# A post-norm decoder layer on one core: row norms moved to ScalarE, recurrence scans joined in pairs, and attention scores of the first rows in two matmuls in place of three

## Time and profile before

| | before |
|---|---|
| median of 3 runs | 1664.29 us (1663.91 to 1665.35) |
| profiled execution, its own time | 1663.39 us |
| its span | 1661.6 us |
| busy PE / PEld | 1571.6 us (95%) / 1424.5 us (86%) |
| busy VectorE | 1389.3 us (84%) |
| busy ScalarE / GpSimd | 1064.8 us (64%) / 995.3 us (60%) |
| granted PE clock, mean | 0.991 |

### The profile page before, as it was taken

How to read it: one execution, slowest core, us unless ns; L and a number is a source line. 1 busy time by engine, 2 the same in 40 slices (tenths; PEclk the granted TensorE clock), 3 DMA queues, 4 the chain that set the end, 5 groups by cost and what they waited for, 6 DMA issues and landing times.

```text
span 1661.6 us, 32864 instructions
## 1 busy us (share of the span) xinstructions
PE 1571.6 (95%) x10720; PEld 1424.5 (86%) x10720; DVE 1389.3 (84%) x3314; ACT 1064.8 (64%) x2883; POOL 995.3 (60%) x856
## 2 busy tenths in 40 slices
PE   5899999999999999999999999999999977989897
PEld 4899989898999999899989998989898966778785
DVE  4555699899989998989899989898989896977874
ACT  4777676767676767676767676767676754233322
POOL 3555566666666666666666666666656652645652
PEclk9999999999999999999999999999999999999999
DMA  7766344424442444244424451445134522112121
GB/s 237 265 197 210 108 134 147 134 58 146 147 134 59 146 146 134 58 140 134 153 56 127 133 169 44 127 139 173 43 121 147 176 57 83 51 66 82 69 77 51
DMA packets 83144, 202.62 MB, mean 122 GB/s; under 512 B 11808, under 2 KB 12832, under 8 KB 82976
## 3 DMA queue, kind: packets, MB, share of 16 engines
q1 hardware_dynamic: 82976, 200.53, 38.6%
HBM read 120.80 MB, written 37.75 MB: 95 GB/s over the span
## 4 chain that ended last, share of the span: by engine, by line
PE 69%; DVE 17%; issue 7%; ACT 3%; POOL 2%; DVEq 1%; SPq 1%; DMA 0%; ACTq 0%; POOLq 0%
PE bank L490 21%; PE bank L492 20%; PE bank L491 20%; PE bank L604 4%; DVE QS L1204 2%; DVE A L1220 2%; DVE PS L1211 1%; DVE S L1069 1%; DVE PTl L1058 1%; DVE RC L1085 1%; PE bank L595 1%; PE bank L587 1%; DVEq L1293 1%; DVE RO L1137 1%; DVE E L1192 1%
## 5 line engine op out<-in xcount | busy, mean ns | idle before, releaser
L490 PE MATMUL bank<-Xh,W 128*128 128x256 f32 x1280 | 362.6, 283 | 36.1 <-DVE RC L1085 26.3
L492 PE MATMUL bank<-Xh,W 128*128 128x256 f32 x1280 | 358.5, 280 | 0.0
L491 PE MATMUL bank<-Xl,W 128*128 128x256 f32 x1280 | 357.7, 279 | 0.0
L946 POOL TENSOR_TENSOR Ql<-RC,Qh 128x512 fp32r<-128x512 f32 x128 | 167.6, 1309 | 266.0 <-ACT Qh L692 265.8
L490 PEld LDWEIGHTS bank<-Xh,W 128*128 128x128 f32 x1280 | 242.1, 189 | 42.9 <-DVE RC L1085 24.2
L692 ACT ACTIVATE PTh<-bank 128x384 fp32r<-128x384 f32 x256 | 125.2, 489 | 211.1 <-PE bank L604 210.7
L692 ACT ACTIVATE S<-S,RL 128x128 f32<-128x128 f32 (+1 forms) x512 | 204.3, 448 | 82.9 <-DVE RL L1077 82.2
L707 ACT ACTIVATE S<-S,NM 128x128 f32<-128x128 f32 (+1 forms) x512 | 227.8, 446 | 40.4 <-DVE NM L1069 39.7
L492 PEld LDWEIGHTS bank<-Xh,W 128*128 128x128 f32 x1280 | 243.0, 190 | 0.0
L491 PEld LDWEIGHTS bank<-Xl,W 128*128 128x128 f32 x1280 | 242.2, 189 | 0.0
L936 POOL TENSOR_TENSOR SW<-SW,tables 128x512 f32<-128x512 f32 x128 | 168.2, 1314 | 116.7 <-DMA SW<-QB 116.2
(11 more groups left out here) (144 smaller groups left out, 4344.2 us busy)
## 6 DMA issues: line engine op xcount, KB each, us to landing
W<-kept SPq DMA_DIRECT2D x140, 512.0 KB, 4.5
SW<-QB SPq DMA_DIRECT2D x256, 128.0 KB, 2.3
kept<-W SPq DMA_DIRECT2D x40, 512.0 KB, 4.5
XR<-in_xt SPq DMA_DIRECT2D x16, 512.0 KB, 4.0
XR<-XR SPq DMA_DIRECT2D x64, 128.0 KB, 2.4
RO<-in_xn SPq DMA_DIRECT2D x16, 512.0 KB, 3.9
KVT<-in_ctxt SPq DMA_DIRECT2D x16, 512.0 KB, 4.3
mixed<-RO SPq DMA_DIRECT2D x16, 512.0 KB, 3.7
```

The lines of the kernel that those rows point to most:

```text
L490: nc.tensor.matmul(dst, lhs[0], rhs[0], start=first, stop=False)
L491: nc.tensor.matmul(dst, lhs[0], rhs[1], start=False, stop=False)
L492: return nc.tensor.matmul(dst, lhs[1], rhs[0], start=False, stop=last)
L946: gp.tensor_tensor(Q[1][:, :, :], RC[:, i % 2, :, :], Q[0][:, :, :], ALU.subtract).then_inc(q_lo, 1)
```

## The change

**Scores.** K's high and low part stand side by side in one tile `KHL`. For rows 0 to 127 one matmul with Q's high part as weights and 2 x 128 columns (128 of K high, 128 of K low) writes columns 0 to 255 of the bank; one with Q's low part adds K high x Q low into columns 0 to 127. The part high x low stays apart in columns 128 to 255. `three` for rows 128 to 255 writes columns 256 to 511. VectorE gets a new instruction per head: the columns 128 to 255 plus mask into S (`masked`); the reduction of the first tile then adds columns 0 to 127 to that, and comes last, after the second tile's.

**Norms.** `norm_apply` goes. VectorE makes -mean*rstd for both row tiles in one 128x2 instruction (`norm_shift`), and ScalarE applies scale and shift in two activations per norm, at the end of the slots with lag 1 and lag 19.

**Scans.** A2, E2, PS and QS have rows of 257 columns with a zero in front, and one scan runs over two channel tiles (514 columns): the zero factor at the border restarts it. Two QS and two PS scans per tail in place of four and four. The memset of PS goes.

**Order.** In odd slots `maxima` stands after the accumulator read; GpSimd's bias adds (line 960) are spread over slots 7, 9 and 11, 13 in place of 9, 11 and 11, 11.

```diff
+QS_AT, PS_AT, ED_AT = [(8, 0), (10, 0)], [(10, 1), (12, 0)], [(6, 0), (9, 0)]
...
-        K = [sb(f"K{i}", [P, 2, JL, T], fr) for i in "hl"]
+        KHL = sb("KHL", [P, 2, JL, 2, T], fr)
+        K = [KHL[:, :, :, i, :] for i in range(2)]
...
+        A2Z = sb("A2Z", [P, KC, T + 1])
+        E2Z = sb("E2Z", [P, KC, T + 1])
+        A2, E2 = A2Z[:, :, 1:T + 1], E2Z[:, :, 1:T + 1]
...
+        in_row = lambda a, h: two(a, h).rearrange("p k t -> p (k t)")
...
-                    for t, c0, keys in ((0, 0, P), (1, P, T)):
-                        last = three(s_ps[:, c0:c0 + keys], [a[:, q, t * P:(t + 1) * P] for a in Q],
-                                     [a[:, par, j, 0:keys] for a in K])
-                    last.then_inc(scored, 1)
+                    nc.tensor.matmul(s_ps[:, 0:2 * P].rearrange("p (i k) -> p i k", i=2), Q[0][:, q, 0:P], KHL[:, par, j, :, 0:P], start=True, stop=False)
+                    nc.tensor.matmul(s_ps[:, 0:P], Q[1][:, q, 0:P], K[0][:, par, j, 0:P], start=False, stop=True)
+                    three(s_ps[:, T:2 * T], [a[:, q, P:T] for a in Q], [a[:, par, j, :] for a in K]).then_inc(scored, 1)
...
+                def norm(kind, tau, rs, nm, done):
+                    act.wait_ge(shifted, SHIFTS.index((kind, tau)) + 1)
+                    rows = RO[:, ro_buf(TAIL_BATCH[tau]), :, :]
+                    for t in range(TT):
+                        last = nc.scalar.activation(rows[:, t, :], rows[:, t, :], ACT.Identity,
+                                                    bias=nm[:, tau % 2, t:t + 1], scale=rs[:, tau % 2, t:t + 1])
+                    last.then_inc(done, 1)
...
-                    b = rows_of(n, 9 + 2 * t, 11)
+                    b = rows_of(n, 7 + 2 * t, 11 + 2 * t)
...
-                    for t, c in ((0, slice(0, P)), (1, slice(P, P + T))):
-                        last = v.tensor_tensor_reduce(out=S[:, i, c], in0=s_ps[:, c], in1=Mask[:, c], scale=-SCALE,
-                                                      scalar=3e38, op0=ALU.add, op1=ALU.min, accum_out=NM[:, i, t:t + 1])
-                    last.then_inc(maxed, 1)
+                    v.tensor_tensor(S[:, i, 0:P], s_ps[:, P:T], Mask[:, 0:P], ALU.add).then_inc(masked, 1)
+                    v.tensor_tensor_reduce(out=S[:, i, P:P + T], in0=s_ps[:, T:2 * T], in1=Mask[:, P:P + T], scale=-SCALE,
+                                           scalar=3e38, op0=ALU.add, op1=ALU.min, accum_out=NM[:, i, 1:2])
+                    dve.wait_ge(masked, g + 1)
+                    v.tensor_tensor_reduce(out=S[:, i, 0:P], in0=s_ps[:, 0:P], in1=S[:, i, 0:P], scale=-SCALE,
+                                           scalar=3e38, op0=ALU.add, op1=ALU.min, accum_out=NM[:, i, 0:1]).then_inc(maxed, 1)
...
-                    last = v.tensor_scalar(tiles[:, t, :], tiles[:, t, :], mv[:, par, t, 0:1], rs[:, par, t:t + 1],
-                                           ALU.subtract, ALU.mult)
+            def norm_shift(par, mv, rs, nm):
+                v.scalar_tensor_tensor(out=nm[:, par, :], in0=mv[:, par, :, 0], scalar=-1.0, in1=rs[:, par, :],
+                                       op0=ALU.mult, op1=ALU.mult).then_inc(shifted, 1)
...
-                    v.tensor_tensor_scan(QS[:, c, 1:T + 1], A2[:, c, :], E2[:, c, :], 0.0, ALU.mult, ALU.add).then_inc(qs_done, 1)
+                        v.tensor_tensor_scan(in_row(QS, h), in_row(A2Z, h), in_row(E2Z, h), 0.0, ALU.mult, ALU.add).then_inc(qs_done, 1)
...
-                    last = v.tensor_tensor_scan(PS[:, c, 1:T + 1], A2[:, c, :], EV[:, c, :], 0.0, ALU.mult, ALU.add)
+                        v.tensor_tensor_scan(in_row(PS, h), in_row(A2Z, h), in_row(E2Z, h), 0.0, ALU.mult, ALU.add).then_inc(ps_done, 1)
```

More of the change, by code:

```diff
@@ L139 @@
             TURNS.append(("y", tail_of(n, T_Y + t), t))
+SHIFTS = []
+for n in range(LAST_SLOT + 1):
+    SHIFTS += [(norm, tail_of(n, lag)) for norm, lag in (("x1", 1), ("x2", T_END - 1)) if tail_of(n, lag) is not None]
 def decoder(nc, xt, xn, ctxt, wraw, bq, bk, bv, bo, wdec, ubon, wf, wl, wb, rw2,
@@ L203, in decoder @@
         QS = sb("QS", [P, KC, T + 1])
-        A2 = sb("A2", [P, KC, T])
-        E2 = sb("E2", [P, KC, T])
+        A2Z = sb("A2Z", [P, KC, T + 1])
+        E2Z = sb("E2Z", [P, KC, T + 1])
+        A2, E2 = A2Z[:, :, 1:T + 1], E2Z[:, :, 1:T + 1]
         ED = sb("ED", [P, KC, T])
         UW = sb("UW", [P, KC])
-        stages = [a[:, 2 * i:2 * i + 2, :].rearrange("p k t -> p (k t)") for a in (KT, VT, A2, E2, ED) for i in range(2)]
         EV = E2
         two = lambda a, h: a[:, 2 * h:2 * h + 2, :]
+        in_row = lambda a, h: two(a, h).rearrange("p k t -> p (k t)")
+        stages = [in_row(a, i)[:, 0:PW] for a in (KT, VT, A2Z, E2Z, ED) for i in range(2)]
         ST = sb("ST", [P, 2, TT, 6])
@@ L221, in decoder @@
         Mhalf = sb("Mhalf", [P, TT])
+        NM1 = sb("NM1", [P, 2, TT])
+        NM2 = sb("NM2", [P, 2, TT])
         w_all = W[:, :, :, :].rearrange("p a i n -> p (a i n)")
@@ L284, in decoder @@
         v_projected, v_hi, v_lo = sem("v_projected"), sem("v_hi"), sem("v_lo")
-        scored, maxed, exped, inverted, normed = (sem(n) for n in ("scored", "maxed", "exped", "inverted", "normed"))
+        scored, masked, maxed, exped, inverted, normed = (sem(n) for n in ("scored", "masked", "maxed", "exped", "inverted", "normed"))
         turned, pt_hi, pt_lo = sem("turned"), sem("pt_hi"), sem("pt_lo")
@@ L800, in exp_a2 @@
                     nc.scalar.activation(two(A2, h), two(A2, h), ACT.Exp, scale=-1.0).then_inc(a2_done, 1)
+                def norm(kind, tau, rs, nm, done):
[5 more added lines that the diff above has]
+                    last.then_inc(done, 1)
+                tau = at(1, 1)
+                if tau is not None:
+                    norm("x1", tau, RS, NM1, x1_done)
+                tau = at(T_END - 1, 1)
+                if tau is not None:
+                    norm("x2", tau, RS2, NM2, x2_done)
                 for t in range(TT):
@@ L1138, in odd @@
                     last.then_inc(acc_read, 1)
+                maxima(n)
                 probabilities(n)
@@ L1171, in tail @@
                     norm_stats(rows(tau), tau % 2, ST, MV, VE, x1_ve)
-                tau = at(1, 1)
+                tau = at(1, 0)
                 if tau is not None:
                     dve.wait_ge(x1_rs, tau + 1)
-                    norm_apply(rows(tau), tau % 2, MV, RS, x1_done)
+                    above(dve, x1_done, tau - 1)
+                    norm_shift(tau % 2, MV, RS, NM1)
                 for tau, c in channels((4, 1), (4, 1), (5, 0), (5, 1)):
@@ L1191, in tail @@
                         above(dve, y_turned, TT * tau)
+                        if tau == 0 and h == 0:
+                            v.memset(A2Z[:, :, 0:1], 0.0)
+                            v.memset(E2Z[:, :, 0:1], 0.0)
                         v.tensor_scalar(two(E2, h), two(KT, h), 0.0, None, ALU.min).then_inc(e2_arg, 1)
                 for h in range(2):
-                    tau = at(6 + 3 * h, 0)
+                    tau = at(*ED_AT[h])
                     if tau is not None:
@@ L1239, in tail @@
                     norm_stats(rows(tau), tau % 2, ST2, MV2, VE2, x2_ve)
-                tau = at(T_END - 1, 1)
+                tau = at(T_END - 1, 0)
                 if tau is not None:
                     dve.wait_ge(x2_rs, tau + 1)
-                    norm_apply(rows(tau), tau % 2, MV2, RS2, x2_done)
+                    above(dve, x2_done, tau - 1)
+                    norm_shift(tau % 2, MV2, RS2, NM2)
             def step(n, part):
```

36 lines of the change are left out of this document (15 added, 21 removed).

## The result

The changed kernel takes 1637.57 us (median of 4, 1636.21 to 1640.59) against 1664.10 (median of 4, 1660.57 to 1665.35) of the kernel before: the ratio is 0.9845, 95% interval 0.983 to 0.9861. That is 26.5 us faster. The prediction was 1632 us, in a range of 1612 to 1652. The total came out nearly right, but the parts do not act as foretold. The scores were to bring 25.6 of the 31.6 us; with the old scores put back, the changed kernel takes about as long as with the new ones. With the old scans put back it loses 18 us.

A forecast was written before the change was run, and what follows sets the result against it. PE sets the pace in 7 slots of 16; in the other 9 PE and VectorE are both full. 1663.4 - 25.6 (scores) - 4 (stalls) - 2 (end stage) = 1631.8; said 1632 us, range 1612 to 1652.

The forecast's parts named there:

- Scores on PE: Each head's score products on PE: five in place of six save 0.10 us, 25.6 us over 256 heads.
- The sum over one tail: Loaded 9 slots: VectorE 1.0 us less, PE 0.9 less, stretch 0.9 shorter; other 7 slots: PE saves 0.7.
- So PE's 25.6 us come through: Conclusion of the tail's sum: PE's whole saving on the scores, 25.6 us, shortens the kernel.
- both engines are full to within 3%, VectorE slightly ahead: Reading of PE and VectorE in the 9 loaded slots, lags 8 to 16 of a tail, before the change.
- Scans: Joined scans on VectorE wait for GpSimd once, taking 1.78 and 1.89 us; saved 2.7 us a tail, 43 in all.
- The added instruction: The mask add on VectorE takes about 0.27 us, costing 0.19 us in the queue, 49 us over 256 heads.
- Norms: Lags 1 and 19: VectorE loses 53 us and gains 5; ScalarE gains 1.55 us a norm, fitting into 1.68 idle.
- Rival 3: ScalarE is late: each of 28 norms in the attention costs PE 0.5 us, +14, giving 1646 us; chance 0.12.
- end stage: After the attention, 9 norm instructions of 0.54 us leave VectorE: 2 us gained (2 lost to 7 gained).
- small shift: 32 small VectorE instructions for the norms, about 0.16 us each: 5 us in all, up to 42 if meeting GpSimd.
- Stalls relieved: Of PE's 22.6 us of waits for VectorE's rotary instruction, 4 us go, outside the loaded lags (none to 18).
- Rival 4: Scans give VectorE 4.4 us a tail; most of the 18 us left of rotary waits vanish: 1614 us; chance 0.15.

The follow-up runs named there:

- split version: Changed kernel with the wide score product cut into two products of 128 columns, VectorE's work unchanged: 1652.0 us, ratio 0.9925 to the kernel before.
- second add: Changed kernel with the mask add done a second time per head into a spare tile, PE unchanged: 1646.4 us, ratio 0.9899 to the kernel before.
- scans spread: Changed kernel with joined scans at lags 9, 10 (QS) and 11, 12 (PS): 1634.7 us; with norms also back on VectorE, 1624.0 us.

## Why the prediction was right, and where it was wrong

**Scores on PE.** Right in size: 0.10 us a head, by the earlier trace rows and the rows after. The reading behind it was incomplete: a narrow product does not always take 0.11 us. The next start is 0.20 us behind the wide product and 0.06 behind the narrow one. The pair costs 0.26 where three products cost 0.36. The split version shows that it is the third product with its weight load, not the columns, that costs.

**The sum over one tail failed.** This is the step that was wrong: "So PE's 25.6 us come through". Scores alone give a ratio of 0.9995 on the kernel before and nothing measurable in the changed one. Of the 23.8 us that the score blocks save over 225 slots, 14.7 come back as waits and 4.4 as wider distances between projection products. The reading that it starts from was too coarse, too: "both engines are full to within 3%, VectorE slightly ahead" holds for the first loaded stretch, but in the second VectorE is busy for 94% and PE for 98%. I compared amounts of work (VectorE 1.0 us less, PE 0.9 us less, so the stretch shortens by 0.9) as if VectorE's time were a fixed sum of durations. Part of it is waiting for GpSimd. That part swallowed a second add of 0.2 us in the loaded stretches, and 0.19 us more at the wrong moment made it longer by 1.1 us.

**Scans.** Their durations came out as foretold (1.71 and 1.87 us), and so did the reason. But I booked their gain only as cover for the mask add; taken out of the changed kernel they cost 18 us, nearly all of it PE's waits (19.0 us over the 225 slots).

**The added instruction.** Its size was right, about 0.2 us in the queue. Charging it at 0.19 us in every slot, covered in the sum by the scans, was wrong: the second add of the same size cost the stretch nothing, while the first, where it lets GpSimd start ahead of a scan, costs 1.1 us at once.

**Norms.** Foretold as a small gain, measured as a loss of 6 us beside the changed kernel, and of 5 to 21 us with the scans spread. The cover on ScalarE held in the attention: 1.9 and 1.1 us in the stretch. Rival 3 priced the loss there at 14 us and was wrong on the place. The profiles put 3.7 and 2.8 us of it in the end stage, where the prediction had 2 us of gain; from before to after that stage grew by 1.2 us. The small shift was sized at 5 us in all, up to 42, and is busy for 18.3.

**Stalls relieved.** 4 us foretold. PE's waits for the rotary instruction went from 15.0 us (190 to 1350 us) to 9.2, and its idle time in the stretch fell by 6.2. Rival 4 had the right mechanism: with the old scores these waits are gone (PE idle 11.5 us). The QS scans moved earlier make them vanish with the new scores too, and the kernel then takes 1630.5 us, not 1614.

**The total** was near partly by luck. From before to after, the score blocks did save the foretold 0.10 us a head and the stalls did shrink, by 6.2 us where 4 were foretold. But the scans, norms and order without the new scores give 0.9853 by themselves, the same as all four parts together (0.9845). The prediction has scores too high by some 22 us and scans too low by some 18. What each part is worth when taken out by itself (3, 18, -6, 0) does not add up to 26.5: a saving on PE and a relief on VectorE do not add where one of them only lengthens or shortens a wait for the other.

**Open:** why the projection products stand 1 ns further apart behind the new scores; what the 6.5 us of waits with the scans spread come from; which wait in the end stage makes ScalarE's norms dearer, and how much dearer; why the second add is paid in the first 33 slots (5.3 of the 6.7 us are PE's waits for the rotary instruction) and absorbed later.

## What to carry to other kernels

Where two engines are both near full, ask of each long instruction what it waits for before counting its duration as work: joining two instructions that each wait for a third engine saves the wait, and a few tenths of a us ahead of such an instruction cost nothing or a whole instruction of the other engine. Take each part of a change out by itself: here one part of four was worth two thirds of the gain, one brought nothing and one cost 6 us. A cheaper product on PE pays in full only where PE waits for nobody.

## What the runs showed of the hardware that was not expected

GpSimd and VectorE wait for each other's whole instruction, in both directions, where VectorE's has two SBUF inputs: 2.14 and 2.21 us for GpSimd instructions of the kind that takes 1.3 otherwise, and 2.35 for a scan that otherwise takes 1.22. Even 2 columns are enough: the shift of 128x2 takes, shortest, median and longest,

```profile
L1181 DVE SCALAR_TENSOR_TENSOR NM<-MV,RS x32: 148/192/1274, 192.9 to 1569.7; 128x2 f32<-128x2 f32 x32
```

The 16 of 32 with a GpSimd instruction in flight at their start end 0.015 to 0.021 us after it; the other 16 take 0.15 to 0.16 us.

Between 20 and 40 us the granted clock of PE, which is either 2.4 or 1.2 GHz, is 0.91 of 2.4 GHz in the mean in the profile before and 0.74 in the one after (PE is busy for 8.9 and 10.4 us of the 20 us ahead, at 1.00); in the version with the order back it is 0.91. Part of the 3.4 us that the start loses can therefore be a difference between runs and not between kernels; this was not isolated. The four runs of the changed kernel with the old scores have mean clocks from 0.984 (span 1645.8 us) to 0.990 (1635.8 us).
